# A two-layer block's expert routing, rewritten: ten 3-bit threshold rounds, candidates on partitions, slot numbers from prefix counts

## What is computed

```python
xf = x.reshape(N, D)
route_prob = jax.nn.softmax(xf @ Ws + bs, axis=-1).T        # 8 x 4096
route_vals, routes = jax.lax.top_k(route_prob, k)            # 8 x 512
xin = xf[routes]
h = jax.nn.gelu(jnp.einsum('ekd,edf->ekf', xin, W1) + b1[:, None, :])
out = jnp.einsum('ekf,efd->ekd', h, W2) + b2[:, None, :]
out = out * route_vals[..., None]
final = jnp.zeros((N, D)).at[routes.reshape(-1)].add(out.reshape(-1, D))
```

## Time and profile before

| | us |
|---|---|
| median of 3 runs | 511.33 |
| lowest and highest | 510.81, 515.11 |
| span of the profiled execution | 518.3 |
| VectorE busy (48%) | 249.2 |
| TensorE busy (63%) | 325.7 |
| GpSimd busy (37%) | 190.8 |
| ScalarE busy (33%) | 170.0 |

### The profile page before, as it was taken

The page is one execution under the profiler, slowest core; times in us unless marked ns, Lnnn a source line. Parts: engine busy times, 40 slices in busy tenths (PEclk is TensorE's granted clock), DMA queues, the critical chain, the costliest instruction groups (busy, mean ns, idle before and its releaser), DMA issues. The chain is left out here.

```text
span 518.3 us, 9527 instructions
## 1 busy us (share of the span) xinstructions
PE 325.7 (63%) x3318; PEld 223.3 (43%) x3318; DVE 249.2 (48%) x986; ACT 170.0 (33%) x263; POOL 190.8 (37%) x208
## 2 busy tenths in 40 slices
PE   3513762888988989799887852211118799867700
PEld 1202441566655656556666631211105366645500
DVE  4461431666667666644756334676777323211100
ACT  1303322656556665553654101000012133222200
POOL 5106500252525353331524031000000768888663
PEclk9655585999999999975999555555555599988955
DMA  7599979979889999996695016700000333433322
GB/s 236 190 188 120 107 78 128 125 146 130 145 127 131 123 139 132 122 140 81 103 131 83 11 30 215 130 0 0 0 2 0 104 70 64 65 63 62 31 21 20
DMA packets 58185, 49.16 MB, mean 95 GB/s; under 512 B 9440, under 2 KB 54832, under 8 KB 57776
## 3 DMA queue, kind: packets, MB, share of 16 engines
q1 hardware_dynamic: 51312, 39.77, 47.7%
q0 software_dynamic: 6848, 9.06, 11.9%
HBM read 15.11 MB, written 8.54 MB: 46 GB/s over the span
## 5 line engine op out<-in xcount | busy, mean ns | idle before, releaser
L483 POOL TENSOR_TENSOR part<-resid,part 128x512 bf16<-128x512 f32 x32 | 38.2, 1194 | 126.4 <-ACT part L590 126.4
L610 ACT ACTIVATE wgt<-ps 128x1024 f32<-128x1024 f32 x64 | 65.2, 1021 | 49.6 <-PE ps L1088 49.5
L546 POOL DMA_INDIRECT area<-token_rows,idx x32 | 31.1, 970 | 96.2 <-DVE idx L1022 86.8
L1072 PE MATMUL ps<-h_t,wqk_sb 128*128 128x512 f32 x64 | 44.1, 778 | 31.6 <-DVE resid L721 23.5
L556 POOL DMA_INDIRECT out_y<-o_sb,idx x32 | 50.4, 1576 | 19.4 <-issue 8.5
L1088 PE MATMUL ps<-area 96*64 96x192 bf16 (+3 forms) x1024 | 51.6, 249 | 4.2 <-issue 2.4
L1115 PE MATMUL ps<-wgt,v_bd 128*32 128x256 f32 (+3 forms) x1024 | 48.6, 338 | 0.0
L1088 PEld LDWEIGHTS ps<-area 96*64 96x64 bf16 x1024 | 38.7, 117 | 18.6 <-issue 17.2
L1115 PEld LDWEIGHTS ps<-wgt,v_bd 128*32 128x32 f32 x1024 | 32.0, 122 | 31.1 <-issue 16.6
L737 DVE SCALAR_TENSOR_TENSOR wgt<-wgt,mask 128x256 f32<-128x256 f32 x64 | 28.9, 452 | 27.6 <-ACT wgt L610 27.6
L721 DVE TENSOR_TENSOR resid<-ps,part 128x512 f32<-128x512 f32 x32 | 21.9, 685 | 39.0 <-ACT part L585 39.0
(11 more groups left out here) (169 smaller groups left out, 543.4 us busy)
## 6 DMA issues: line engine op xcount, KB each, us to landing
area<-part SPq DMA_DIRECT2D x192, 128.0 KB, 4.6
modb<-mod_rows SPq DMA_DIRECT2D x3, 1024.0 KB, 6.6
token_rows<-area POOLq DMA_DIRECT2D x1, 2048.0 KB, 25.9
out_y<-x SPq DMA_DIRECT2D x16, 128.0 KB, 3.8
token_rows<-h SPq DMA_DIRECT2D x16, 128.0 KB, 3.9
xall<-in_w SPq DMA_DIRECT2D x1, 2048.0 KB, 9.1
modb<-in_w SPq DMA_DIRECT2D x8, 256.0 KB, 7.8
xall<-in_x SPq DMA_DIRECT2D x2, 576.0 KB, 6.8
```

Of the source, the lines that this page charges most:

```text
L483: nc.gpsimd.tensor_tensor(part[buf][2][:, :], resid[buf][:, :], part[buf][1][:, :], ALU.subtract)\
L546: eng.indirect_dma_start(out=xg[e % 4][:, j, :], out_offset=None, in_=rows[:, :], in_offset=bass.IndirectOffsetOnAxis(ap=idx[:, e, j:j + 1 ...
L610: nc.scalar.activation(wgt[sp][:, 2 * half:2 * half + 2, :], ps[:, 2 * half:2 * half + 2, :], ACT.Square, scale=0.25, bias=1.0).then_inc(s ...
L1072: mm(ps[:, B_FR, :], wqk_sb[:, gi, :], h_t[:, :], start=True, stop=True).then_inc(s_qkp, 1)
```

## The change

It replaces everything between `pr` and `idx`.

- **Layout.** `pr` is written eight times over as `pr_rep` (tokens of a tile, expert, candidate), half by VectorE, half by ScalarE, and 16 transposes turn it into `p_all` [2 token halves x 8 experts x 8 candidates on 128 partitions, 2048 tokens]. The first 1024 columns also go to `p_odd`, with the last bit set.
- **Search.** Ten rounds fix three bits of the threshold's bit pattern each. In a round each partition compares with its own candidate: VectorE counts columns 1024 to 2047 of `p_all`; ScalarE counts the first 1024 as a sum of signs over `p_odd`. Two accumulating matmuls with the counts as weights add both over the token halves and give every partition all 64 totals. VectorE counts the candidates that reached 512, and ORs the result into `base`. The last round has no ScalarE part and counts all 2048 columns on VectorE.
- **Slots.** `pick` has the tie marks beside the chosen marks. 32 bf16 matmuls count them along the partitions (`upto`, `after`), two small ones along the tiles. `begun` marks for each tile the slots at or behind its first. 64 matmuls over 32 rows each (32 for each half of the experts) give for every slot the running counts of its own tile and, in the last column, the tile. VectorE counts how many lie below the slot number (`count_inside`, four instructions an expert) and puts `idx` together.
- The routing constants are others. TensorE's first transposes and matmuls of experts 0 and 1 also wait for the `idx` that free their PSUM banks.

```diff
             def routing_constants():
-                nc.gpsimd.memset(blk[:, :], 0.0)
-                nc.gpsimd.memset(upper[:, :], 1.0)
...
-                nc.gpsimd.iota(iota_i, pattern=[[1, 32], [0, NT]], base=0, channel_multiplier=0).then_inc(s_ci, 1)
...
+                nc.gpsimd.memset(own2[:, :, :, :], 1.0)
+                nc.gpsimd.memset(blk32[:, :], 1.0)
+                nc.gpsimd.memset(upto[:, :], 1.0)
+                nc.gpsimd.memset(after[:, :], 1.0)
...
+                nc.gpsimd.affine_select(out=blk32[:, :], in_=blk32[:, :], compare_op=ALU.is_ge, fill=0.0, base=0,
+                                        pattern=[[-32, 4], [0, 32]], channel_multiplier=1)
...
@@ scalar @@
             eng.wait_ge(s_pr, 1)
+            nc.scalar.activation(pr_rep[:, NT // 2:NT, :, :],
+                                 pr[:, :, NT // 2:NT].rearrange("p e t -> p t e").unsqueeze(3)
+                                 .broadcast_to([P, NT // 2, NE, NC]), ACT.Copy).then_inc(s_rep[1], 1)
             nc.scalar.activation(pr_te[:, :, :].rearrange("p t e -> p e t"), pr[:, :, :], ACT.Copy).then_inc(s_pte, 1)
-            for e in range(NE):
-                eng.wait_ge(s_ohh, e + 1)
...
+            for n in range(2, 4):
+                eng.wait_ge(s_ptp, n + 1)
+                nc.scalar.activation(p_all[:, 512 * n:512 * n + 512], ps[:, n, :], ACT.Copy).then_inc(s_pall, 1)
+            for n in range(len(SHIFTS) - 1):
+                eng.wait_ge(s_podd, 2)
+                eng.wait_ge(s_bs, n + 2)
+                nc.scalar.activation(signs, p_odd, ACT.Sign, scale=-1.0, bias=base[:, 1:2].bitcast(fp32),
+                                     accum_out=cnt_s[:, :]).then_inc(s_cns, 1)
+                if n < 2:
+                    nc.scalar.activation(p_all[:, 512 * n:512 * n + 512], ps[:, n, :], ACT.Copy).then_inc(s_pex, 1)
...
@@ vector @@
+            for n, shift in enumerate(SHIFTS):
+                last = n == len(SHIFTS) - 1
...
+                nc.vector.tensor_scalar(hits[:, c0:], p_all[:, c0:], base[:, 1:2].bitcast(fp32), 0.0, ALU.is_ge, ALU.add,
+                                        accum_out=cnt[:, :]).then_inc(s_cnt, 1)
...
+                eng.wait_ge(s_tot, n + 1)
+                nc.vector.scalar_tensor_tensor(reached[:, :], ps[:, 4, 0:NE * NC], float(CAP if last else CAP - NACT),
+                                               own[:, :], ALU.is_ge, ALU.mult, accum_out=steps_up[:, :])                    .then_inc(s_rch, 1)
+                eng.wait_ge(s_rch, n + 1)
+                nc.vector.tensor_scalar(delta[:, :], steps_up[:, :], -1.0, 2.0 ** shift, ALU.add, ALU.mult)                    .then_inc(s_dl, 1)
...
+            def count_inside(e):
+                eng.wait_ge(s_sl, e // 4 + 1)
+                for j in range(CT):
+                    k = nc.vector.tensor_scalar(low[:, e % 2, j, 0:P - 1], ps[:, SLOT_BANK[e], j * P:(j + 1) * P - 1],
+                                                slot[:, j:j + 1], -float(P), ALU.is_le, ALU.add,
+                                                accum_out=inside[:, e, j:j + 1])
+                k.then_inc(s_in, 1)
...
@@ tensor @@
+            for n in range(len(SHIFTS)):
+                last = n == len(SHIFTS) - 1
+                if not last:
+                    eng.wait_ge(s_cns, n + 1)
+                    mm(ps[:, 4, 0:NE * NC], cnt_s[:, 0:1].broadcast_to([P, P]), fold_s[:, :], start=True, stop=False)
+                eng.wait_ge(s_cnt, n + 1)
+                mm(ps[:, 4, 0:NE * NC], cnt[:, 0:1].broadcast_to([P, P]), fold[:, :], start=last, stop=True)                    .then_inc(s_tot, 1)
...
+                for j in range(CT):
+                    for a in range(2):
+                        for q in range(4):
+                            g = 2 * a + h
+                            k = mm(ps[:, SLOT_BANK[4 * h + q], j * P:(j + 1) * P],
+                                   begun[32 * q:32 * q + 32, g, j * P:(j + 1) * P],
+                                   pick_t[32 * q:32 * q + 32, g, :], start=(a == 0), stop=(a == 1))
+                k.then_inc(s_sl, 1)
```

More of the change, by code:

```diff
@@ L176, in adaln_block_kernel @@
[L176 to L186, removed]
@@ L198, in adaln_block_kernel @@
-        idx_s = sb("idx_s", [P, NE, 16], i32)
+        cnt = sb("cnt", [P, 1], fp32)
+        cnt_s = sb("cnt_s", [P, 1], fp32)
+        reached = sb("reached", [P, NE * NC], fp32)
+        steps_up = sb("steps_up", [P, 1], fp32)
+        delta = sb("delta", [P, 1], i32)
+        next_base = sb("next_base", [P, 2], i32)
+        base = sb("base", [P, 2], i32)
+        digits = sb("digits", [P, len(SHIFTS)], i32)
+        part_i = sb("part_i", [P, 1], i32)
+        fold = sb("fold", [P, NE * NC], fp32)
@@ new lines, in adaln_block_kernel @@
+        fold_s = sb("fold_s", [P, NE * NC], fp32)
+        own = sb("own", [P, NE * NC], fp32)
+        sel = sb("sel", [P, NE], fp32)
+        thr_sel = sb("thr_sel", [P, NE], fp32)
+        blk32 = sb("blk32", [P, P], bf16)
+        before32 = sb("before32", [P, P], bf16)
+        upto = sb("upto", [P, P], bf16)
+        after = sb("after", [P, P], bf16)
+        slot = sb("slot", [P, CT], fp32)
+        slot_i = sb("slot_i", [P, CAP], mybir.dt.int16)
+        pick = sb("pick", [P, 2, 4, 2 * NT + 1], bf16)
@@ new lines, in _ @@
+            nc.vector.memset(base[:, 0:1], 0)
+            nc.vector.tensor_copy(base[:, 1:2], digits[:, 0:1]).then_inc(s_bs, 1)
+            eng.wait_ge(s_pr, 1)
+            nc.vector.tensor_copy(pr_rep[:, 0:NT // 2, :, :],
+                                  pr[:, :, 0:NT // 2].rearrange("p e t -> p t e").unsqueeze(3)
+                                  .broadcast_to([P, NT // 2, NE, NC])).then_inc(s_rep[0], 1)
+            for n in range(2):
+                eng.wait_ge(s_ptp, n + 1)
+                nc.vector.tensor_scalar(p_odd[:, 512 * n:512 * n + 512].bitcast(i32), ps[:, n, :].bitcast(i32), 1, None,
+                                        ALU.bitwise_or).then_inc(s_podd, 1)
@@ new lines, in _ @@
+            k.then_inc(s_pick, 1)
+            eng.wait_ge(s_ptk, 1)
+            nc.vector.tensor_copy(n_tile[:, :], ps[:, 2, P - 1:512:P]).then_inc(s_nt, 1)
+            eng.wait_ge(s_fp, 1)
+            nc.vector.tensor_copy(first[:, :], ps[:, 3, 0:4]).then_inc(s_first, 1)
+            eng.wait_ge(s_first, 1)
+            for h in range(2):
+                for a in range(2):
+                    g = 2 * a + h
+                    k = nc.vector.tensor_scalar(begun[:, g, :], slot_i[:, :], first[:, g:g + 1], None, ALU.is_ge)
+                k.then_inc(s_beg, 1)
```

327 lines of the change are left out of this document (135 added, 192 removed).

## The result

| us | before | after |
|---|---|---|
| median (4 executions each) | 513.22 | 479.33 |
| lowest and highest | 510.81, 517.65 | 476.99, 483.40 |
| span of the profiled execution | 518.3 | 477.6 |
| ratio after / before | | 0.934, 95% 0.926 to 0.942 |

It is faster by 6.6% (5.8 to 7.4).

A forecast was written before the change was run, and what follows sets the result against it. The 81.2 us routing ladder from `pr` to the first gather was taken as the bound. 518.3 - 31.0 - 0.5 + 0.4 = 487.2 for the profiled execution; against the median, 511.33 - 31.1 = 480.2 us, range 472 to 489.

The forecast's parts named there:

- setup: From `pr` ready to round 0: copies into `pr_rep`, sixteen transposes and ScalarE's last bank copy, 5.3 us.
- nine rounds: Search rounds with VectorE and ScalarE both counting and two matmuls in a row: 3.2 us each, 28.8 in all.
- last round: Final search round, VectorE comparing all 2048 elements at the slow rate, one matmul: 3.85 us.
- threshold to first gather: Selection, picks, count matmuls, `begun`, slot matmuls, `count_inside` and hand-over to GpSimd: 12.3 us.
- first gather to `x_copy`: Seven experts' `idx` work before VectorE starts `x_copy`: 8.65 us after the gather instead of 9.2, 0.5 gained.
- constants: GpSimd's routing constants about 2.4 us longer, first `low_part` up to 0.9 late; 0.4 taken as reaching the end.
- The faster compare: By the skill's two elements a cycle, the last round would be 1.07 us shorter, giving 479.1 instead of 480.2.
- The 32 count matmuls: Between threshold and first gather: 0.074 us each as in L1115, 2.4 in all; upper end 0.233 each.
- The 32 slot matmuls: Between `begun` and `count_inside`: 0.11 us each, 3.7 with start and hand-over; ends 0.074 and 0.233 each.
- Slow small matmuls: Rival: both groups of 32 at L1260's 0.233 us each and `begun` slower, total 489.7; chance 0.12.
- The clock granted in the routing: Rival: TensorE at 2.4 GHz during the routing shortens rounds, counts, slots and expert 0, total 471; chance 0.07.
- Slower, or hardly paying: Two rivals: ScalarE's sum of signs far dearer, 516, chance 0.02; rounds of 6 us by stalls, 506, chance 0.03.

The follow-up runs named there:

- the second profile of the changed kernel: The changed kernel itself, unedited, run again beside the kernel with ScalarE's share at 832 columns: 479.21 us, ratio 0.933.
- the price experiment: The changed kernel with seven groups of 16 small matmuls added ahead of expert 0's transposes, to time one matmul of each form: 496.85 us, one execution.
- the fill in the drained unit and behind the slots: The changed kernel with unread 512-column matmuls added in the drained last unit, the rounds, around the slots and behind them: 478.74 us, ratio 0.934.
- 26 us of fill in the rounds: The changed kernel with four unread 512-column matmuls added behind each search round's own: 477.42 us, ratio 0.929.
- e9_share832: The changed kernel with ScalarE comparing 832 columns instead of 1024 in nine rounds, VectorE 192 more: 475.68 us, ratio 0.921; again 474.68, ratio 0.925.

## Why the prediction was right, and where not

Its own steps, from `pr` ready (316.68 in the profile of after):

| step | predicted | measured |
|---|---|---|
| setup | 5.3 | 5.0 |
| nine rounds | 28.8 (3.2 each) | 27.9 (2.55, then 8 x 3.17) |
| last round | 3.85 | 3.8 |
| threshold to first gather | 12.3 | 8.0 |
| first gather to `x_copy` | 8.65 | 8.1 |
| constants | +0.4 | 0 |

**The bound** was right: the routing's ladder was all on the path, and the tail stayed as it was (94.4 and 95.0).

**Rounds.** Each price held: compare 1.28, accumulator 0.08, ScalarE 1.15 and 0.19, two matmuls 1.13, `reached` 0.31. The accumulator's read on ScalarE, for which the earlier trace rows gave only bounds, was at the value taken. Round 0 was 0.6 shorter, since its matmuls ran at 2.4 GHz (0.41 and 0.22 instead of 0.69 and 0.43). This differs between executions: of the ten profiles with the new search the clock was up in round 0 in five. In the second profile of the changed kernel it was at 0.50 there, and the search took 37.7 instead of 37.1.

**The faster compare** did not come. The compare of 2048 took 2.35, which is 0.21 and 1.04 ns an element, as the row of 343 ns had said. The Trainium skill (VectorE: DVE Perf Modes, "The perf-mode tier table") gives this kind of operation two elements a cycle; the trace does not agree for the form with an accumulator.

**Threshold to gather** is the term that was mis-sized, by 4.3. Selection, picks, small steps, `begun`, `count_inside` and the hand-over to GpSimd were within 0.2 each. Two terms make 4.0 of it:
- The 32 count matmuls took 1.1 with hand-over instead of 2.55. I took L1115's 0.074 as "the same form". But that row is fp32, its 32 entries are the passes of 16 matmuls, and the merged row shows only the largest of four widths. Before's groups by form, the largest and the smallest:

```profile
L1115 PE MATMUL ps<-wgt,v_bd 128*32 128x256 f32 x256 | 23.5, 444 | 0.0
L1115 PE MATMUL ps<-wgt,v_bd 128*32 128x64 f32 x256 | 10.2, 234 | 0.0
```

  The widths 256, 192, 128 and 64 occur equally often. A price for 128 bf16 columns could not be read off it. An fp32 pass of 128 columns in turns is 0.053 in the price experiment; the count matmuls, in bf16, were (1.05 - 0.33) / 31 = 0.023 apart.
- The 32 slot matmuls took 1.1 to their reader instead of 3.7. The 0.11 was right for one matmul of this size (0.105 in the price experiment). What was missing is that four row groups in turn run beside each other: (1.89 - 0.31) / 63 = 0.025 each. I had L1115's 0.074 as the lower end, misread as above, so that end was too high as well.

**Constants** cost nothing. I had priced each new select at 0.83, the time of before's only one. In the changed kernel the first select took 1.19 and the ones behind it 0.18 to 0.41. All constants took 6.8 us (53.44 to 60.23) instead of 6.1 (52.67 to 58.79) before, 0.7 longer and not 2.4, and the first `low_part` still found 0.92 of slack.

**The sum and the time.** The routing saved 81.2 - 44.7 = 36.6, 5.6 more than the 31.0 of the sum, and `x_copy` 1.1 instead of 0.5. (By the sum's own terms 0.4 would have been due: 9.65 less 0.84 is 8.8, not 8.65.) So the mechanism was right and the size of the saving was not, and that the time hit within 0.9 is in part luck. The medians differ by 513.22 - 479.33 = 33.9, 2.8 more than the 31.1 forecast, but the median subtracted from, 511.33 of three executions, was 1.9 lower than the 513.22 of four; the two errors nearly cancel. The kernel before had medians of 513.6 to 518.8 in the later comparisons. Between the 37.7 us that the stages give and the 33.9 of the medians lies scatter in the attention and the first expert; the interval of the ratio, 30 to 38 us, covers both. The 7 us between the profiled execution and the median were scatter too, not the price of the profile: the device time of the profiled execution of after, 479.34, is its span and 1.7 more.

**The rivals.** Slow small matmuls: excluded, they were faster than in my case, and what spoke against that rival (the stride) is now shown. The clock granted in the routing: it was for 3.4 us of it (320.7 to 324.1), worth 0.6, and in no round behind that, with and without fill. The Trainium skill (TensorE: Matmul & The Clock Gate, "What's actually happening") has activity release the gate; the fill in the drained unit and behind the slots (clock 1.00 and 0.80) agrees, 26 us of fill in the rounds (0.50) do not. Slower, or hardly paying: ScalarE's row was 1.15, and the straight-line rounds show no stall.

## What to carry to other kernels

Before a row's price is used for a new matmul, compare its moving columns, its type, the stride of its moving operand and whether neighbours lie in different groups of 32 rows or columns: here the type was worth a factor of 2 for a full-size matmul (0.215 for an fp32 transpose, 0.105 in bf16), the stride 2.2, and the groups 4 to 5 (0.106 against 0.02 to 0.025). A merged row can hide several shapes: ask for the groups by form before dividing. When two engines split a count that a third collects one after the other, let the one whose result is collected first be ready earlier (collecting it takes 0.48 us here), not at the same time; by the trace that gave 0.17 a round. Cut both profiles at the same events of the program before taking differences: here the changed stages repeat to 0.2 us where the clock is the same, while the attention ahead of them moves by several us between executions.

## What the hardware showed that I had not expected

- Matmuls of 32 rows or 32 output columns in bf16 in turns of four groups follow each other at 0.02 to 0.025 us at 1.2 GHz, and within one group at 0.106. Even with eight of one group in a row two groups ran beside each other (3.86 for 64).
- A moving operand with an element every 32 bytes costs 0.234 a matmul, at 2.4 GHz as measured here, and L1260's with one every 64 bytes 0.233 at 1.2 GHz; the plain form takes 0.105 at 1.2 GHz. A strided stationary operand costs nothing.
- Engines stood still while the gathers were under way, in code where nothing that they wait for was missing, as far as the profile shows. In the price experiment it was TensorE, 6.3 us "issue" in all within the fourth group, between 375.0 and 383.2. In eight of the thirteen profiles, of both kernels and of their variants, it was VectorE and ScalarE: they start again together 22.7 to 23.0 us after the first gather, 2.2 to 3.6 us after the matmuls that VectorE waits for have ended. TensorE's stall ended 22.6 after the first gather. Timeline of e9_share832, and last the same step of the changed kernel, which starts at once:

```profile
371.79 3.84 PE L1294 MATMUL ps<-modb,area 128*128 128x128 f32 x32 [0.34 <-issue]
379.07 0.69 DVE L1027 TENSOR_TENSOR area<-ps,b_sb 128x512 f32<-128x512 f32 x1 [6.89 <-remote]
379.11 2.42 ACT L705 ACTIVATE area<-ps,b_sb 128x512 f32<-128x512 f32 x4 [7.37 <-PE ps L1284]
...
381.05 0.69 DVE L1024 TENSOR_TENSOR area<-ps,b_sb 128x512 f32<-128x512 f32 x1 [3.49 <-PE ps L1291]
```

  This is why the third stage is 21 to 23 us in some profiles and 25 in others. The profiles of before and after that were compared first are both without it. The cause is open, and no run was made to find it.
- `begun`, int16 to bf16 with a scalar per partition, took 1.14 for four times 512 elements, one every 0.27, faster than the 0.48 worked out from fp32 rows.
